# Hand-over from attention to the experts: last three tiles in an order of their own, row numbers spread by TensorE, the first expert's rows turned by groups

## The reference

```python
x = x + tanh(g_xattn[0]) * softmax(mask((q @ k.T) * scaling * layernorm(x)))   # q, k from ctx_512
# experts: E = 64, K = 8, H = 1024, I = 384, CAP = 256
logits = layernorm(x) @ gate_w.T
probs = softmax(logits)
w, sel = top_k(probs, K);  w = w / sum(w)
pos = cumsum(one_hot(sel)) - 1 ;  valid = pos < CAP         # place of a token at its expert
inp[e, pos] = layernorm(x)[token]                           # at most CAP rows an expert
h = silu(inp[e] @ wg[e]) * (inp[e] @ wu[e])
out[e] = h @ wd[e]
x = x + tanh(g_ffn[0]) * sum over the 8 chosen of w * out[e, pos] (only if valid)
```

## Time and profile before

| | us |
|---|---|
| median of 3 runs | 1880.2 (1880.05 to 1880.25) |
| the profiled execution | 1881.87 |
| its span | 1880.1 |
| first product of expert 0 starts at | 357.98 |
| first product of expert 1 starts at | 388.40 |
| PE busy / DVE busy / ACT busy / POOL busy | 1793.4 / 1452.0 / 1230.3 / 1064.2 |

### The profile page before, as it was taken

One profiled execution on the slowest core, in us unless ns is written; L12 is line 12 of the kernel. 1 busy time (PEld: TensorE's weight loads), 2 busy tenths in 40 slices (PEclk: granted clock), 3 DMA queues, 4 the chain that ended last, 5 costly groups with the idle time before them and its releaser, 6 DMA issues.

```text
span 1880.1 us, 36989 instructions
## 1 busy us (share of the span) xinstructions
PE 1793.4 (95%) x12929; PEld 1310.6 (70%) x12993; DVE 1452.0 (77%) x2529; ACT 1230.3 (65%) x1795; POOL 1064.2 (57%) x817
## 2 busy tenths in 40 slices
PE   6989987499999999999999999999999999999997
PEld 2655655367777777777777777777777777777775
DVE  3989997677777777777777777777777777777773
ACT  4988986466666666666666666666666666666662
POOL 1000000666666666666666666666666666666651
PEclk9999997699999999999999999999999999999998
DMA  6577553499999999999999999999999999999992
GB/s 212 183 270 287 196 208 127 136 297 303 301 303 300 301 303 301 302 301 302 302 299 302 302 301 302 301 302 302 301 300 302 302 303 300 301 301 302 301 296 45
DMA packets 90072, 516.96 MB, mean 275 GB/s; under 512 B 16816, under 2 KB 19376, under 8 KB 64944
## 3 DMA queue, kind: packets, MB, share of 16 engines
q1 hardware_dynamic: 46304, 357.59, 48.4%
q0 software_dynamic: 43008, 151.04, 34.7%
q10 hardware_dynamic: 720, 7.86, 1.2%
HBM read 409.21 MB, written 107.22 MB: 275 GB/s over the span
## 4 chain that ended last, share of the span: by engine, by line
PE 87%; DVE 6%; DMA 2%; issue 2%; ACT 2%; POOL 1%; SPq 0%; POOLq 0%; DVEq 0%; ACTq 0%
PE ps_gu L474 53%; PE ps_d L483 26%; PE ps_s L393 3%; PE ps_l L411 2%; PE ps_j L382 2%; DMA xb<-in_x 1%; POOL xg L1077 1%; PE ps_t L403 1%; DVE zb L742 1%; DVE xb L898 1%; DVE zb L770 1%; DVE at L804 1%; DMA h_rows<-hrow 1%; DMA b_qk<-in_bqT 0%; DVE at L810 0%
## 5 line engine op out<-in xcount | busy, mean ns | idle before, releaser
L1077 POOL DMA_INDIRECT xg<-h_rows,g_idx x512 | 727.4, 1421 | 191.0 <-issue 133.0
L474 PE MATMUL ps_gu<-xT,split_g 128*128 128x256 bf16 x4608 | 536.2, 273 | 24.1 <-DVE xT L972 24.1
L474 PE MATMUL ps_gu<-xT,split_u 128*128 128x256 bf16 x4608 | 534.4, 273 | 0.0
L474 PEld LDWEIGHTS ps_gu<-xT,split_g 128*128 128x128 bf16 x4608 | 451.7, 98 | 90.9 <-issue 24.4
L483 PE MATMUL ps_d<-split_d,act 128*128 128x512 bf16 x2240 | 495.4, 380 | 6.8 <-DVE act L961 3.5
L474 PEld LDWEIGHTS ps_gu<-xT,split_u 128*128 128x128 bf16 x4608 | 450.9, 98 | 52.2
L483 PEld LDWEIGHTS ps_d<-split_d,act 128*128 128x128 bf16 x2304 | 225.7, 98 | 262.8 <-issue 5.6
L676 ACT ACTIVATE ob<-ps_d,wcol 128x512 f32<-128x512 f32 x256 | 171.3, 687 | 346.8 <-PE ps_d L483 346.8
L1097 POOL DMA_INDIRECT out<-ob,s_idx x128 | 205.1, 1603 | 301.6 <-ACT ob L676 215.1
L967 DVE STREAM_TRANSPOSE xt<-xg 128x512 f32<-128x512 f32 x256 | 166.5, 688 | 163.1 <-DMA xg<-h_rows,g_idx 163.1
L951 DVE TENSOR_TENSOR split_d<-raw_d,split_d 128x1536 bf16<-128x1536 f32 x128 | 219.3, 1754 | 75.8 <-ACT split_d L653 75.7
(11 more groups left out here) (96 smaller groups left out, 1373.0 us busy)
## 6 DMA issues: line engine op xcount, KB each, us to landing
raw_d<-in_wd SPq DMA_DIRECT2D x63, 1536.0 KB
raw_g<-in_wg SPq DMA_DIRECT2D x62, 1536.0 KB
raw_u<-in_wu SPq DMA_DIRECT2D x62, 1536.0 KB, 16.0
h_rows<-hrow SPq DMA_DIRECT2D x34, 640.0 KB, 3.4
xb<-in_x SPq DMA_DIRECT2D x32, 512.0 KB, 4.5
out<-xb SPq DMA_DIRECT2D x32, 512.0 KB, 3.5
xg<-h_rows,g_idx POOLq DMA_INDIRECT x512
...
```

Of the source, the lines that this page charges most:

```text
L474: mm = pe.matmul(ps_gu[m][:, t, :], w[:, wi, k, m * P:(m + 1) * P], xT[u][:, k, xi, :], start=(k == 0 and (wi, xi) == (0, 0)), stop=(k == ...
L1077: p.indirect_dma_start(out=xg[u][:, g, :], out_offset=None, in_=h_rows, in_offset=bass.IndirectOffsetOnAxis(ap=g_idx[u][:, g:g + 1].bitcas ...
```

## The change

Six things change, all around the hand-over; the loops over the experts 2 to 63 and the tiles 0 to 29 keep their instructions.

1. **Last tiles.** The loop over tiles ends at g = 30; what is left of the last tiles is written out on TensorE, ScalarE and VectorE in an order of its own. The row weights of the last three tiles are applied by ScalarE (`row_shares`) instead of VectorE.
2. **Idle products.** TensorE gets products that nobody reads: 16 + 8 + 8 + 24 of 128 columns (`idle_turns`) in the last tiles, and 40 of 256 columns (`marks`) ahead of expert 0, ten behind each of the last four groups of turned rows.
3. **Row numbers.** `table_f` is the table in floating point; TensorE multiplies it by four constant matrices (`spread`, made by POOL at the start), and one VectorE instruction makes `g_idx[0]` from the result (`ps_x`), one more the whole `piece_table`. POOL waits only for `g_idx[0]` before the first gather, and its copy of a column is gone for expert 0.
4. **First rows by groups.** Each of the eight fetches has its own semaphore; VectorE turns a group (128 x 256) as it lands, ScalarE and VectorE split it.
5. **Order of expert 0.** On ScalarE and VectorE its own down weights and the splitting of expert 1's weights come in a written-out order; the function table for Silu is loaded by a one-element Silu at the start.
6. The semaphore counts of `turned`, `xT_high` and `xT_out` start with expert 1.

The diff, cut to its core (12 columns of indentation taken off, semaphore and tile declarations left out):

```diff
@@ TensorE, end of attention @@
+def idle_turns(n):
+    for _ in range(n):
+        pe.matmul(ps_j[:, 0:P], ones[:], ones[:], start=True, stop=True)
+pe.wait_ge(proj_out, 8 * B)
+positions(N - 3)
+places(N - 5)
+turn_h(N - 2)
+idle_turns(16)
+logits(N - 2)
+turn_h(N - 1)
+places(N - 4)
+positions(N - 2)
+idle_turns(8)
+logits(N - 1)
+places(N - 3)
+positions(N - 1)
+counts()
+idle_turns(8)
+places(N - 2)
+idle_turns(24)
+places(N - 1)
+pe.wait_ge(spread_made, 1)
+pe.wait_ge(pos_used, N)
+pe.wait_ge(table_made, 1)
+for a in range(QS):
+    mm = pe.matmul(ps_x[:, a].rearrange("p h e -> p (h e)"), spread[:, a], table_f[:].rearrange("p h e -> p (h e)"),
+                   start=True, stop=True)
+mm.then_inc(spread_done, 1)
...
@@ TensorE, ahead of expert(0) @@
+marks = ident[:].bitcast(BF16)
+for g in range(4, NG):
+    pe.wait_ge(first_turned, g)
+    for _ in range(10):
+        pe.matmul(ps_d[3][:, 0:2 * P], marks[:, 0:P], marks, start=True, stop=True)
...
@@ ScalarE, last tiles @@
+def row_shares(g):
+    s.wait_ge(shares_ready, g - (N - 4))
+    s.wait_ge(routed, g)
+    s.activation(hrow[g % 4][:, :, QH:QW], ew[g % 2][:].unsqueeze(1).to_broadcast([P, QS, E]), ACT.Copy,
+                 scale=r8[:, g % 2, 1:2]).then_inc(routed, 1)
+x1_square(N - 1)
+turned_out(N - 2)
+expert_weights(N - 3)
+normalize(N - 1)
+row_shares(N - 3)
+turned_out(N - 1)
+expert_weights(N - 2)
+row_shares(N - 2)
+expert_weights(N - 1)
+row_shares(N - 1)
...
@@ ScalarE, first expert @@
+def first_high_part(g):
+    ts = slice(g * 32, (g + 1) * 32)
+    s.wait_ge(first_turned, g + 1)
+    s.activation(xT[0][:, :, 0, ts], xt[:, :, ts], ACT.Copy).then_inc(first_high, 1)
...
-for part in range(2):
-    gate_high(0, 0, part, True)
-for part in range(2):
-    up_high(0, 0, part, True)
-for q in range(4):
-    turned_high(0, 0, q)
-weights(0, 0)
-expert(0, 0, True)
+def first_expert():
+    s.activation(ob[1][:, 0, 0:1], ident[:, 0:1], ACT.Silu).then_inc(silu_table, 1)
+    for part in range(2):
+        gate_high(0, 0, part, True)
+    for part in range(2):
+        up_high(0, 0, part, True)
+    for g in range(5):
+        first_high_part(g)
+    down_high(0, 0, True)
+    first_high_part(5)
+    down_high(0, 1, True)
+    first_high_part(6)
+    first_high_part(7)
+    s.wait_ge(silu_table, 1)
+    weights(0, 0)
+    gate_high(1, 1, 0, True)
+    gate_high(1, 1, 1, True)
+    up_high(1, 1, 0, True)
+    silu(0, 0)
+    up_high(1, 1, 1, True)
+    silu(0, 1)
+    for q in range(4):
+        turned_high(1, 1, q)
+    weights(1, 1)
+    silu(0, 2)
+    rows_out(0, 0, True)
+first_expert()
...
@@ VectorE, last tiles @@
+def steps(of, g, n):
+    for _ in range(n):
+        next(of[g])
+steps(added, N - 1, 3)
+steps(routes, N - 5, 1)
+steps(weighted, N - 5, 1)
+steps(routes, N - 3, 1)
+x1_variance(N - 1).then_inc(var_ready, 1)
+steps(routes, N - 3, 5)
+steps(weighted, N - 4, 3)
+minus_mean1(N - 1)
+steps(routes, N - 4, 2)
+steps(weighted, N - 3, 2)
+steps(picks, N - 2, 5)
+steps(routes, N - 3, 2)
+steps(routes, N - 2, 6)
+steps(weighted, N - 2, 2)
+steps(picks, N - 1, 5)
+steps(routes, N - 2, 2)
+steps(weighted, N - 1, 2)
+steps(routes, N - 1, 8)
...
@@ VectorE, the tables @@
+v.scalar_tensor_tensor(table_f[:], ps_w[:, 0], MID, fill[:], ALU.add, ALU.add).then_inc(table_made, 1)
+v.wait_ge(spread_done, 1)
+v.wait_ge(quarters_made, QS)
+v.tensor_scalar(g_idx[0][:].rearrange("p (h a) -> p a h", a=QS), ps_x[:, :, :, 0], float(QS), quarter_no[:],
+                ALU.mult, ALU.add).then_inc(first_pieces, 1)
 v.wait_ge(table_made, 1)
-for q in range(QS):
-    for part in range(QS):
-        v.tensor_scalar(piece_table[q * 32:(q + 1) * 32, part::QS], table[part * 32:(part + 1) * 32],
-                        float(QS), float(q), ALU.mult, ALU.add).then_inc(pieces_made, 1)
+v.tensor_copy(table[:], table_f[:]).then_inc(pieces_made, 1)
+v.tensor_scalar(piece_table[:].rearrange("p (h a) e -> p a h e", a=QS), ps_x[:], float(QS), quarter_no[:],
+                ALU.mult, ALU.add).then_inc(pieces_made, 1)
...
@@ VectorE, first expert @@
+def first_turn(g):
+    v.wait_ge(first_rows[g], 16)
+    v.transpose(xt[:, :, g * 32:(g + 1) * 32], xg[0][:, g, 0:QH].rearrange("p (b i) -> p b i", i=32)
+                ).then_inc(first_turned, 1)
+def first_low_part(g):
+    ts = slice(g * 32, (g + 1) * 32)
+    v.wait_ge(first_high, g + 1)
+    v.tensor_tensor(xT[0][:, :, 1, ts], xt[:, :, ts], xT[0][:, :, 0, ts], ALU.subtract).then_inc(first_low, 1)
+def first_expert():
+    gate_low(0, 0, 0)
+    gate_low(0, 0, 1)
+    for g in range(3):
+        first_turn(g)
+    up_low(0, 0, 0)
+    first_turn(3)
+    for g in range(3):
+        first_low_part(g)
+    first_turn(4)
+    first_low_part(3)
+    up_low(0, 0, 1)
+    first_turn(5)
+    first_low_part(4)
+    first_low_part(5)
+    first_turn(6)
+    first_low_part(6)
+    first_turn(7)
+    first_low_part(7)
+    down_low(0, 0)
+    down_low(0, 1)
+    gate_low(1, 1, 0)
+    activate(0, 0, 0, True)
+    gate_low(1, 1, 1)
+    up_low(1, 1, 0)
+    for q in range(4):
+        turn(1, 1, q)
+    activate(0, 0, 1, True)
+    turned_low(1, 1, 0)
+    turned_low(1, 1, 1)
+    up_low(1, 1, 1)
+    activate(0, 0, 2, True)
+    turned_low(1, 1, 2)
+    turned_low(1, 1, 3)
...
@@ GpSimd @@
+p.tensor_copy(spread[:].rearrange("p a (q r) -> p a q r", r=32),
+              ident[:].rearrange("p (a r) -> p a r", r=32).unsqueeze(2).to_broadcast([P, QS, QS, 32])
+              ).then_inc(spread_made, 1)
...
-p.wait_ge(pieces_made, QS * QS)
+p.wait_ge(first_pieces, 1)
...
+def first_gather():
+    hold()
+    for g in range(NG):
+        p.indirect_dma_start(
+            out=xg[0][:, g, :], out_offset=None, in_=h_rows,
+            in_offset=bass.IndirectOffsetOnAxis(ap=g_idx[0][:, g:g + 1].bitcast(U32), axis=0),
+            bounds_check=last_piece, oob_is_err=True,
+        ).then_inc(first_rows[g], 16)
...
-gather(0, 0)
+first_gather()
+p.wait_ge(pieces_made, 2)
 gather(1, 1)
```

More of the change, by code:

```diff
@@ L114, in flamingo_moe @@
         piece_table = sb("piece_table", [P, NG, E], I32)
+        table_f = sb("table_f", [P, 2, E], F32)
+        spread = sb("spread", [P, QS, P], F32)
+        quarter_no = sb("quarter_no", [P, 1], F32)
+        g_idx = [sb(f"g_idx{u}", [P, NG], I32) for u in range(2)]
         a_mem = ExitStack()
@@ L449, in _ @@
                     places(g - 4)
[L450 removed]
+                if g >= 1:
                     turn_h(g - 1)
@@ L605, in _ @@
             project_out(1, 0)
-            for g in range(N + 2):
+            for g in range(N - 1):
                 if g + 2 < N:
```

146 lines of the change are left out of this document (81 added, 65 removed).

## The result

| | before | after |
|---|---|---|
| median, us | 1881.39 (1880.05 to 1887.02, 10 runs) | 1875.43 (1870.47 to 1878.09, 10 runs) |
| profiled execution, span | 1881.87, 1880.1 | 1874.99, 1873.2 |
| expert 0, expert 1 start at (chain) | 357.98, 388.40 | 348.97, 381.70 |

The ratio is 0.9963 (95% interval 0.9951 to 0.9975), faster by 6.0 us, or 0.4%. 1870.3 was forecast, with a range of 1864.5 to 1875.5, so the measured time lies 0.07 us inside its upper end. In the profiled executions 6.9 us went, and 6.7 of them ahead of expert 1. (The chain puts the start of expert 1 0.16 us later than PE's timeline, which has 388.24 and 381.54.)

A forecast was written before the change was run, and what follows sets the result against it. PE bounds the unchanged expert loop, so only expert 1's earlier start counts: 4.3 + 1.4 + 4.1 - 0.1 + 0.2 = 9.9 us, profiled 1881.87 to 1872.0, median 1.7 lower: 1870.3 us, range 1864.5 to 1875.5.

The forecast's parts named there:

- rival (d): Loop over the experts: each pass grows as moved buffers shift its phase to the loads; at 0.3 us, 1889; chance 0.07.
- (b): Last tiles: the clock stays down, so the gain is only 4 to 5.5 us, about 1875.5; chance 0.13.
- (c): Both gathers: group turning and early numbers make POOL and DVE obstruct each other, losing 3.5 us, 1873.8; chance 0.12.
- Step 1: Last tiles: new order and idle products raise PE's clock, last logits end near 321.75; 4.3 us earlier.
- Step 2: Last logits to the table: row weights go to ACT and DVE's wait for PE's last places goes; 1.4 us.
- Step 3: Table to first gather: TensorE products and one DVE instruction make the row numbers, 3.0 us instead of 7.1; 4.1 us.
- Step 4: First gather to expert 0: group turning's gain is spent on POOL issues waiting for subtractions; 16.7 us against 16.6, nothing.
- Step 5: Expert 0: a faster gate and up is lost waiting for expert 1's rows, then cold down products; nothing gained.
- Rival (a): Expert 0: expert 1's rows land early, expert 1 starts at 374.4, 14.0 us gained, 1866.2; chance 0.23.

The follow-up runs named there:

- e2: Changed kernel without the 56 idle products of the last tiles (the 40 ahead of expert 0 stay): 1877.24 us.
- e7: Kernel before the change, with only 16 and 8 idle TensorE products added ahead of the logits of its last two tiles: 1881.39 us, ratio 0.9993.
- e8: Changed kernel with the row numbers made as before (16 VectorE instructions and GpSimd's copy, no TensorE products for them): 1876.74 us.
- e6: Changed kernel with each weight subtraction in expert 0's stretch on VectorE cut into four pieces: 1873.15 us.
- e10: e1 with expert 0's gate and up subtractions cut into quarters and ScalarE's down splits behind all high parts of expert 0's rows: 1864.47 us.
- e1: Changed kernel with expert 0's second and third activation ahead of expert 1's four turns on VectorE, and Silu ahead of expert 1's high parts on ScalarE: 1866.85 us.
- e3: Changed kernel without the 40 idle products ahead of expert 0: 1874.61 us.
- e4: Changed kernel, but SyncE issues the weight loads behind expert 0 only when expert 1's rows have landed: 1870.48 us.
- e9: Changed kernel with expert 0's rows turned only when all eight groups have landed, ScalarE splitting all groups ahead of the down weights: 1873.44 us.
- e11: Changed kernel, but expert 0 behind its group turns in the old order on VectorE and ScalarE, weight loads behind them: 1873.11 us.

## Why the prediction was right, and where it was off

The mechanism held: all of the gain lies ahead of expert 1, the loop is unchanged (rival (d) is out), and the worth of the change is read from expert 1's start. The sum was 9.9 us, the two profiled executions differ by 6.9. The number was right by a hair: 1875.43 lies at the very end of the range, outside the band of the forecast itself (1868 to 1872.5), and the range reached that far only for rivals (b) and (c), whose mechanisms are not, or only in part, what happened. That it fell inside is luck; that the chain of waits came as foretold is not.

- **Step 1, right, its size in part by luck.** 4.3 us forecast, 4.4 measured (the copy of the logits at 321.60 instead of 326.02). Places, turn and idle products lie within 0.3 us of the text. But the clock was up with tile 30's logits already (1.95 us, not 2.6), and the last logits ended at 321.11, the bound for a clock that rises at once, 0.6 us ahead of the forecast; VectorE was still busy then and copied them 0.5 us later. The two errors cancel. e2 shows that the idle products raise the clock, e7 that they do it without the new order too. Rival (b), a clock that stays down, is what e2 makes: 4.0 us of gain from the anchor to expert 1, where 4 to 5.5 were priced.
- **Step 2, over by 0.9.** The table came 4.9 us earlier, so 0.5 instead of 1.4 is this step's. PE's clock was down again for the last places (0.95 us at 327.98), and DVE still waited 0.59 us for them where I had put nothing. The other 0.3 us are mostly the row weights: in before the next instruction starts 0.27 us behind each of the three, so taking them away gives 0.8 us and not 1.0.
- **Step 3, right.** 4.1 forecast, 4.4 measured (2.7 us from table to first issue); e8 gives the same 4.4 by undoing it. The products took 1.13 us, 0.28 each, for which I had taken 0.4.
- **Step 4, right in size.** Expert 0 starts 16.9 us behind the first gather, 16.7 were said; the gather's issues end at 345.31, 345.1 were said. The waits for subtractions are shown by e6, but not that they alone eat the gain (1.6 us by the text): without them expert 0 still starts at 16.9 us. Only with ScalarE's down splits moved as well (e10) does it start earlier, 16.2 us against 17.6 in e1.
- **Step 5 failed in size.** It said that expert 0 would cost what it did before; it cost 2.3 us more. Its chain is the one that happened: rows land late beside the weight loads, turns, activation, stop, cold down products. But the 13.7 us from the loads' issue to the rows came out as 14.8 (13.0 to 14.1 in e8, e3 and e2), the loads started 0.5 us later than said, from the landing to down it took 4.4 us instead of 3.8, and down took 10.18 us instead of 9.2. The stop of PE was 6.68 us instead of 5.4. The forecast took one meeting in the trace of before as the size of another: there the last issue began 6.2 us behind the load's, in after 6.5, and the rows come later when it does. How much of the 1.1 us this is, and how much scatter, the single traces don't tell. Down was cold for longer: the granted clock stayed at 0.50 until about 376.5, 5.0 us behind its start, in before for some 3.0 us; why is open. Added up: 9.9 us, 0.1 and 0.3 more by steps 1 and 3, 0.9, 0.2 and 2.5 less by steps 2, 4 and 5, is 6.7.
- **Rival (a)** was named for the right reason: had the rows been early, expert 1 would have been at 374.4. e4, in which they are, took 25.0 us for expert 0 instead of 32.6. **Rival (c)**, that turning by groups and early numbers only let the engines stand in each other's way, is half right, and its price (1873.8) is nearer to the measured time than the forecast is: steps 4 and 5 lost 2.7 us where it had 3.5. The numbers pay at the gather; the groups, the idle products ahead of expert 0 and its new order show no gain (e9, e3, e11), each by traces of one execution and by medians that can't be told from that of after.

What the steps did not ask is the question that was worth the most: why down waits for expert 1's rows. They followed the written order and priced it; e1 moved two activations and took off 8.9 us from the anchor to expert 1, more than the whole change. On Silu's function table the Trainium skill ("ScalarE: Activation LUTs", What ACT_TABLE_LOAD costs) adds a drain of about 1.38 us; after shows none, the load runs from 329.43 to 330.71 and Silu starts at 330.73.
